# Causal attention: the running maxima of 128 and 256 columns taken for four or two heads in one bank

## Chip, core and metric

One NeuronCore of a Trainium2 chip (trn2) runs the whole program in one launch. The metric is device time in microseconds (us), from the first to the last instruction of the core with what the runtime puts around it. The kernel before took 1778.22 us in the median of 3 runs (1775.87 to 1778.82).

## The reference, cut to what matters

The program is a chain of six layers on x of 4 batches x 1024 tokens x 128 features: a routed feed-forward layer, causal attention, the same feed-forward layer again, a second kind of routed feed-forward layer, a gated attention unit, and that feed-forward layer again. The change is in the causal attention alone:

```
qkv = layernorm(x) @ w_in.T + b_in          # 16 heads of width 8
scores = einsum('bhqd,bhkd->bhqk', q / sqrt(8), k) + causal_bias
attn = softmax(scores, axis=-1)             # exp(score - row maximum) / sum
out = einsum('bhqk,bhkd->bhqd', attn, v) @ w_out.T + b_out
```

The row maximum of each query is needed before the exponentials. The kernel therefore computes the scores twice: once with queries on the partitions, from which VectorE takes the maxima over the keys, and once with keys on the partitions, from which ScalarE takes the exponentials.

## The kernel before, in words

**Sections.** Attention is cut into 16 sections (4 batches x 4 groups of HG = 4 heads). In a section the queries and keys of four heads lie in `q_st` (128 rows of contraction, 1024 queries; the four heads stand in rows of their own) and `k_pad` (one padded copy of the keys for each head j, zero in the other heads' rows). So one stationary tile of 128 queries serves all four heads, and the head is chosen by which `k_pad[:, n % 2, j, ...]` streams past it.

**The maxima (lines 865 to 870, `peak` at 1039 on TensorE and at 1276 on VectorE).** A block (t, c) is the product of query tile t (8 tiles of 128) with key half c (512 keys); only the causal part is computed, `width_of(t, c)` columns: 128, 256, 384 and 512 for t = 0 to 3 and again for t = 4 to 7 in half 1, and 512 for t = 4 to 7 in half 0. That is 12 blocks for each head, 48 in a section. MAXB packs them into 9 PSUM banks for each head, 36 in a section: six blocks stand alone, three banks hold two blocks (128 with 384, twice, and 256 with 256). TensorE issues one weight load and one matmul for each block (line 1049).
**The ring.** These banks, and those of the projections, transposes and the output product, come from a ring of RING = 3 PSUM banks. `fill` (line 978) makes TensorE wait until the bank three entries back has been emptied, `content` (line 985) makes the consumer wait for the fill. Both engines take their instructions strictly in the order of the program.

**The rest of a section.** TensorE also issues the second score products (`score`, line 1068, 12 units of key block and query half for two pairs of heads), the products with v (`pv`, line 1087, two units later), the transposes of the output (`ot`, 1096), and once a batch (four sections) the normalised input's transposes (1013), projections (1019 to 1021), the output transposes (1103) and the output product (`wo`, 1110). ScalarE takes the exponentials (1157), GpSimd zeroes the diagonal (1197). Behind the last maximum of a section VectorE forms the negated maximum in three dependent steps (`neg`, 1294 to 1301), TensorE transposes it (`maxt`, 1058) and a DMA puts it into rows of `q_st`. Once a batch VectorE has the two steps of `wo` (1319 to 1327), each a chain of three operations.

**The order.** `order()` (line 876) gives every step a due time in units of a section and sorts; all engines walk that one list. The maxima of section n run beside the scores of section n - 1 and are spread evenly:

```
put(n - 1.18 + 0.93 * (i * HG + j) / (len(MAXB) * HG), "max", n, j, i)
put(at(g) + pair * weight[u] / sum(weight) / 2, "score", n, u, pair)   # begin[u]: 0, .104, .188, .25, .292, .396, ...
put(at(g + 2) + 0.001, "pv", n, u)
```

The maxima of section 0 have no scores beside them. Those of section 15 are the last; behind them only the scores of section 15 are left.

Of the kernel before, what the change touches and what calls it, by code (L numbers as in the profile page):

```python
# [9 lines left out]
ALU = mybir.AluOpType  # L10
# [838 lines left out]
def phase_attention(nc, k, own, a, begun, lead):  # L849
# [15 lines left out]
    MAXB = (((3, 0),), ((4, 0),), ((5, 0),), ((6, 0),), ((7, 0),), ((0, 0), (2, 0)),  # L865
            ((7, 1),), ((4, 1), (6, 1)), ((1, 0), (5, 1)))
    HALF1 = next(i for i, parts in enumerate(MAXB) if any(c > 0 for _, c in parts))

# [7 lines left out]
    def order():  # L876
# [13 lines left out]
        for n in range(SECTIONS):  # L890
# [14 lines left out]
            for i in range(len(MAXB)):  # L905
                for j in range(HG):
                    put(n - 1.18 + 0.93 * (i * HG + j) / (len(MAXB) * HG), "max", n, j, i)
# [27 lines left out]
    for entry in ORDER:  # L935
        if entry[0] in SMALL:
            if ("max", SECTIONS - 1, HG - 1, len(MAXB) - 1) in SLOT and n % RING == LENT:
                n += 1
            SLOT[entry] = n
            n += 1  # L940
    TAKEN_UP = sum(n % RING == LENT for n in SLOT.values())

    with ExitStack() as ctx:
# [27 lines left out]
        neg_steps, max_in = sem("neg_steps"), sem("max_in")  # L971
# [35 lines left out]
        def _(pe):  # L1007
# [31 lines left out]
            def peak(n, j, i):  # L1039
                bank, full = fill(pe, "max", n, j, i)  # L1040
                at = 0
                if i == 0 and j == 0:
                    pe.wait_ge(q_in[n % 3], 16 * 2 * (n // 3 + 1))
                    pe.wait_ge(k_in[n % 2][0], 16 * HG * (n // 2 + 1))
                if i == HALF1 and j == 0:
                    pe.wait_ge(k_in[n % 2][1], 16 * HG * (n // 2 + 1))
                for t, c in MAXB[i]:
                    width = width_of(t, c)
                    mm = pe.matmul(bank[:, at:at + width], q_st[:, n % 3, t * P:(t + 1) * P],  # L1049
                                   k_pad[:, n % 2, j, c * G:c * G + width], start=True, stop=True,  # L1050
                                   skip_group_check=True)
                    at += width
                mm.then_inc(full, 1)
# [194 lines left out]
        def _(dve):  # L1248
# [27 lines left out]
            def peak(n, j, i):  # L1276
                bank, empty = content(dve, "max", n, j, i)
                if n > 0 and i == 0 and j == 0:
                    dve.wait_ge(neg_steps, 3 * n - 2)
                at = 0  # L1280
                for t, c in MAXB[i]:
                    width = width_of(t, c)
                    now, best = bank[:, at:at + width], mx[:, j, 2 * t + c:2 * t + c + 1]
                    if c == t // TG:
                        ins = dve.tensor_tensor_reduce(now, now, mask[:, G - width:G], 1.0, -3e38, ALU.add, ALU.max, best)  # L1285
                    else:
# [681 lines left out]
```

## Time and profile before

| | before |
|---|---|
| median of 3 runs | 1778.22 us |
| the profiled execution's own time | 1777.67 us |
| its span (first to last instruction) | 1775.7 us |
| attention: first maximum to last exponential product, about | 242 to 830 us |
| TensorE busy | 1644.0 us, 93% of the span |
| VectorE busy | 1289.3 us, 73% |
| ScalarE busy | 1016.6 us, 57% |
| GpSimd busy | 774.5 us, 44% |

A matmul's time in the profile goes from its start to a modelled end and overlaps with the next one's, so a busy TensorE is not one at its peak: the distance from one start to the next (here called the pitch) is what an instruction costs in a row of its kind. The same holds for VectorE, whose instructions overlap a little with the next. The profiled execution lies 0.55 us below the median of the runs.

### The profile page before, as it was taken

To read this page: it belongs to the slowest core of one execution; us is meant where nothing else is said; L and a number is where in the kernel's file an instruction comes from. 1 tells how busy PE (TensorE), PEld (TensorE's weight loads), DVE (VectorE), ACT (ScalarE), POOL (GpSimd) and SP (SyncE) were. 2 spreads that over 40 slices of the span, in tenths; PEclk is the share of its full clock that TensorE was granted. 3 is DMA by queue.
4 is the path that set the end of the run, shared out by engine and by line. 5 is a ranking of instruction groups with operands and counts; after the bars stand their busy time and mean duration, and the time that the engine had idled before them with its cause. 6 is when DMAs were issued, how large, how long until landed. Compare 5 with 4: busy or idle time off the path is not lost. (4 is left out here: it accounts for less than half of the span.)

```text
span 1775.7 us, 25917 instructions
## 1 busy us (share of the span) xinstructions
PE 1644.0 (93%) x8360; PEld 1149.7 (65%) x8360; DVE 1289.3 (73%) x3879; ACT 1016.6 (57%) x1718; POOL 774.5 (44%) x734
## 2 busy tenths in 40 slices
PE   3999879899999999998999999999998988999998
PEld 2777645555555555554777767777777876777776
DVE  4777668788778878883777767777766876767775
ACT  3666415565566566566666645555555645555554
POOL 1566611311311311212566646555574615555555
PEclk9999969999999999999999999999999998999999
DMA  4222211011111111101233332111110002111120
GB/s 149 74 91 84 93 33 35 16 24 25 21 30 24 20 22 28 30 11 38 79 121 120 103 95 88 54 49 48 49 48 1 1 1 90 60 55 60 55 94 19
DMA packets 58246, 95.01 MB, mean 54 GB/s; under 512 B 9312, under 2 KB 17120, under 8 KB 58112
## 3 DMA queue, kind: packets, MB, share of 16 engines
q1 hardware_dynamic: 56000, 91.07, 18.2%
q10 hardware_dynamic: 2112, 2.30, 0.4%
q8 instruction: 66, 1.08, 0.3%
q14 instruction: 68, 0.56, 0.1%
HBM read 76.76 MB, written 2.88 MB: 45 GB/s over the span
## 5 line engine op out<-in xcount | busy, mean ns | idle before, releaser
L695 DVE TENSOR_TENSOR big<-banks,big 128x512 f32<-128x512 f32 x384 | 264.4, 689 | 214.7 <-ACT banks L632 179.8
L1157 ACT ACTIVATE big<-banks 128x1024 f32<-128x1024 f32 (+3 forms) x384 | 304.3, 810 | 187.9 <-PE banks L1068 182.5
L632 ACT ACTIVATE banks<-banks 128x512 f32<-128x512 f32 x384 | 224.0, 583 | 277.3 <-PE banks L575 272.1
L705 DVE TENSOR_TENSOR big<-big,banks 128x512 f32<-128x512 f32 x400 | 274.7, 687 | 29.8 <-PE banks L578 15.9
L1049 PE MATMUL banks<-arena 128*128 128x512 f32 (+3 forms) x768 | 251.9, 407 | 32.2 <-DVE att_mx L1285 15.4
L1285 DVE CUSTOM_DVE_ANT_0 banks<-banks,att_mask 128x128 f32<-128x128 f32 (+3 forms) x512 | 235.6, 521 | 52.2 <-PE banks L1049 51.6
L1197 POOL TENSOR_SCALAR_AFFINE_SELECT big<-big 128x512 f32<-128x512 f32 x128 | 81.2, 635 | 402.5 <-ACT big L1157 402.5
L1049 PEld LDWEIGHTS banks<-arena 128*128 128x128 f32 x768 | 136.6, 199 | 162.3 <-issue 98.2
L665 POOL TENSOR_TENSOR ffn1b_hid_l<-big,ffn1b_hid_h 128x512 fp32r<-128x512 f32 x128 | 165.5, 1293 | 128.3 <-ACT ffn1b_hid_h L637 128.3
L665 POOL TENSOR_TENSOR ffn1a_hid_l<-big,ffn1a_hid_h 128x512 fp32r<-128x512 f32 x128 | 165.2, 1291 | 118.0 <-ACT ffn1a_hid_h L637 118.0
L575 PE MATMUL banks<-xh,arena 128*128 128x512 f32 x512 | 208.7, 408 | 7.9 <-PEq L1451 6.8
L578 PE MATMUL banks<-xh,arena 128*128 128x512 f32 x512 | 203.2, 397 | 0.0
L1068 PE MATMUL banks<-arena 128*128 128x512 f32 (+3 forms) x768 | 200.7, 351 | 2.0 <-ACT big L1157 1.8
L1287 DVE TENSOR_REDUCE att_mx<-banks 128x1 f32<-128x512 f32 x256 | 164.1, 683 | 26.3 <-PE banks L1049 26.2
L1087 PE MATMUL banks<-big,att_v_aug 128*32 128x512 f32 (+3 forms) x1536 | 165.8, 504 | 0.6 <-POOL big L1197 0.5
L1068 PEld LDWEIGHTS banks<-arena 128*128 128x128 f32 x768 | 136.4, 191 | 24.2 <-ACT big L1157 9.2
L665 POOL TENSOR_TENSOR ffn0a_hid_l<-big,ffn0a_hid_h 128x512 fp32r<-128x512 f32 x72 | 92.7, 1289 | 85.6 <-ACT ffn0a_hid_h L637 85.5
L665 POOL TENSOR_TENSOR ffn0b_hid_l<-big,ffn0b_hid_h 128x512 fp32r<-128x512 f32 x72 | 93.0, 1291 | 63.5 <-ACT ffn0b_hid_h L637 62.9
L575 PEld LDWEIGHTS banks<-xh,arena 128*128 128x128 f32 x512 | 97.3, 190 | 29.5 <-issue 8.7
L578 PEld LDWEIGHTS banks<-xh,arena 128*128 128x128 f32 x512 | 97.0, 189 | 22.3
L578 PE MATMUL banks<-xl,arena 128*128 128x512 f32 x256 | 101.7, 397 | 0.0
L575 PE MATMUL banks<-xl,arena 128*128 128x512 f32 x256 | 101.1, 395 | 0.0
(256 smaller groups left out, 3153.7 us busy)
## 6 DMA issues: line engine op xcount, KB each, us to landing
big<-weight_rows SPq DMA_DIRECT2D x256, 128.0 KB, 3.0
big<-weight_rows SPq DMA_DIRECT2D x128, 256.0 KB, 4.3
arena<-att_parts SPq DMA_DIRECT2D x16, 384.0 KB
arena<-att_parts SPq DMA_DIRECT2D x128, 48.0 KB
w_raw<-in_ffn_w_dram SPq DMA_DIRECT2D x12, 256.0 KB, 3.0
out_dram<-x SPq DMA_DIRECT2D x8, 256.0 KB, 2.3
setup_raw<-in_ffn_w_dram SPq DMA_DIRECT2D x3, 576.0 KB, 6.9
gau_angle<-in_consts_dram SPq DMA_DIRECT2D x2, 512.0 KB, 7.3
```

The costliest lines, as they stand in the source:

```text
L575: mm = pe.matmul(gate_ps[:, num % NB, :], w[:, ws], xx[:, g % 2, :], start=m == 0, stop=m == 2)
L578: mm = pe.matmul(up_ps[:, num % NB, :], w[:, ws], xx[:, g % 2, :], start=m == 0, stop=m == 2)
L632: act.activation(gate if c < NSCALED else sil, gate, ACT.Silu).then_inc(silu_done, 1)
L665: pool.tensor_tensor(hid_l[:, num % NH, :], hid[:, num % NH, :], hid_h[:, num % NH, :].bitcast(F32), ALU.subtract).then_inc(low_cut, 1)
L695: dve.tensor_tensor(scl[:, num % 2, :], gate_ps[:, num % NB, :], share[:, c // PER, :], ALU.mult)\
L705: dve.tensor_tensor(hid[:, num % NH, :], scl[:, num % 2, :] if c < NSCALED else sil, up_ps[:, num % NB, :], ALU.mult).then_inc(hidden, 1)
L1049: mm = pe.matmul(bank[:, at:at + width], q_st[:, n % 3, t * P:(t + 1) * P], k_pad[:, n % 2, j, c * G:c * G + width], start=True, stop=True ...
L1068: mm = pe.matmul(score_ps[:, pair, h, 0:c], k_pad[:, n % 2, 2 * pair + h, kb * P:(kb + 1) * P], q_st[:, n % 3, (qg + 1) * G - c:(qg + 1) * ...
L1087: mm = pe.matmul(o_ps[32 * j:32 * j + 32, G - c:G], v_aug[:, b % 2, kb, at:at + 32], probs[:, unit % NPROB, j, 0:c], start=kb == 0, stop=k ...
L1157: act.activation(probs[:, unit % NPROB, 2 * pair:2 * pair + 2, 0:c], score_ps[:, pair, :, 0:c], ACT.Exp, scale=SCALE).then_inc(exped, 1)
L1285: ins = dve.tensor_tensor_reduce(now, now, mask[:, G - width:G], 1.0, -3e38, ALU.add, ALU.max, best)
L1287: ins = dve.tensor_reduce(best, now, AX.X, ALU.max)
```

## The change

Every MAXB entry is now one block for a set of heads: one head (ONE), two (TWO) or all four (ALL). The blocks of 128 columns are taken for all four heads at once (4 x 128 = 512 columns), those of 256 for two heads at once, those of 384 and 512 for each head alone. TensorE issues one matmul for an entry, whose moving operand runs over the heads' copies of the keys. VectorE treats one-head entries as before. A merged entry gets two operations: `tensor_tensor` adds the mask to the last 128 columns of each head in place in the bank, and after a wait on its own semaphore `edged` one `tensor_reduce` over the whole bank gives the maxima of all its heads. A section has 38 entries (32 of one head, 4 of two, 2 of four) in place of 36 banks, in a new order, evenly spread again over 0.93 of a section. `neg` waits for the last three entries.

```diff
--- before.py
+++ after.py
@@ -862,9 +862,12 @@
     LOW, AGAIN = (1, 2), (2, 1)
 
 
-    MAXB = (((3, 0),), ((4, 0),), ((5, 0),), ((6, 0),), ((7, 0),), ((0, 0), (2, 0)),
-            ((7, 1),), ((4, 1), (6, 1)), ((1, 0), (5, 1)))
-    HALF1 = next(i for i, parts in enumerate(MAXB) if any(c > 0 for _, c in parts))
+    ONE, TWO, ALL = [(j, j + 1) for j in range(HG)], [(j, j + 2) for j in range(0, HG, 2)], [(0, HG)]
+    MAXB = [(t, c, heads) for t, c, sets in
+            ((3, 0, ONE), (4, 0, ONE), (5, 0, ONE), (0, 0, ALL), (6, 0, ONE), (1, 0, TWO), (7, 0, ONE), (2, 0, ONE),
+             (7, 1, ONE), (4, 1, ALL), (6, 1, ONE), (5, 1, TWO)) for heads in sets]
+    MERGED = sum(b - a > 1 for _, _, (a, b) in MAXB)
+    HALF1 = next(i for i, (_, c, _) in enumerate(MAXB) if c > 0)
 
     def width_of(t, c):
         return min(G, (t + 1) * P - c * G)
@@ -903,8 +906,7 @@
             for h in range(HALF):
                 put(n - 1.34 + 0.34 * h, "keys", n, h)
             for i in range(len(MAXB)):
-                for j in range(HG):
-                    put(n - 1.18 + 0.93 * (i * HG + j) / (len(MAXB) * HG), "max", n, j, i)
+                put(n - 1.18 + 0.93 * i / len(MAXB), "max", n, i)
             put(n - 0.255, "neg", n)
             put(n - 0.15, "maxt", n)
             for u in range(NU):
@@ -934,7 +936,7 @@
     SLOT, n = {}, 0
     for entry in ORDER:
         if entry[0] in SMALL:
-            if ("max", SECTIONS - 1, HG - 1, len(MAXB) - 1) in SLOT and n % RING == LENT:
+            if ("max", SECTIONS - 1, len(MAXB) - 1) in SLOT and n % RING == LENT:
                 n += 1
             SLOT[entry] = n
             n += 1
@@ -968,7 +970,7 @@
         emptied = [sem(f"emptied{n}") for n in range(RING)]
         moments, eps_done, rstd_done, norm_done = begun.moments, begun.eps_done, begun.rstd_done, begun.norm_done
         xh_done, qk_high, qk_again = sem("xh_done"), sem("qk_high"), sem("qk_again")
-        neg_steps, max_in = sem("neg_steps"), sem("max_in")
+        neg_steps, max_in, edged = sem("neg_steps"), sem("max_in"), sem("edged")
         q_in = [sem(f"q_in{p}") for p in range(3)]
         k_in = [[sem(f"k_in{p}{h}") for h in range(HALF)] for p in range(2)]
         scored, exped, masked = sem("scored"), sem("exped"), sem("masked")
@@ -1036,21 +1038,18 @@
                 bank, full = fill(pe, "proj", b, w, h)
                 three(bank, full, w_h[:, w, :], w_l[:, w, :], h)
 
-            def peak(n, j, i):
-                bank, full = fill(pe, "max", n, j, i)
-                at = 0
-                if i == 0 and j == 0:
+            def peak(n, i):
+                bank, full = fill(pe, "max", n, i)
+                t, c, (j0, j1) = MAXB[i]
+                if i == 0:
                     pe.wait_ge(q_in[n % 3], 16 * 2 * (n // 3 + 1))
                     pe.wait_ge(k_in[n % 2][0], 16 * HG * (n // 2 + 1))
-                if i == HALF1 and j == 0:
+                if i == HALF1:
                     pe.wait_ge(k_in[n % 2][1], 16 * HG * (n // 2 + 1))
-                for t, c in MAXB[i]:
-                    width = width_of(t, c)
-                    mm = pe.matmul(bank[:, at:at + width], q_st[:, n % 3, t * P:(t + 1) * P],
-                                   k_pad[:, n % 2, j, c * G:c * G + width], start=True, stop=True,
-                                   skip_group_check=True)
-                    at += width
-                mm.then_inc(full, 1)
+                width = width_of(t, c)
+                pe.matmul(bank[:, 0:(j1 - j0) * width].rearrange("p (j w) -> p j w", w=width),
+                          q_st[:, n % 3, t * P:(t + 1) * P], k_pad[:, n % 2, j0:j1, c * G:c * G + width],
+                          start=True, stop=True, skip_group_check=True).then_inc(full, 1)
 
             def maxt(n):
                 bank, full = fill(pe, "maxt", n)
@@ -1273,24 +1272,30 @@
                 dve.scalar_tensor_tensor(parts[:, w, LOW[w], cut], bank, b_in[:, w:w + 1], parts[:, w, 0, cut].bitcast(F32),
                                          ALU.add, ALU.subtract).then_inc(empty, 1)
 
-            def peak(n, j, i):
-                bank, empty = content(dve, "max", n, j, i)
-                if n > 0 and i == 0 and j == 0:
+            def peak(n, i):
+                bank, empty = content(dve, "max", n, i)
+                t, c, (j0, j1) = MAXB[i]
+                if n > 0 and i == 0:
                     dve.wait_ge(neg_steps, 3 * n - 2)
-                at = 0
-                for t, c in MAXB[i]:
-                    width = width_of(t, c)
-                    now, best = bank[:, at:at + width], mx[:, j, 2 * t + c:2 * t + c + 1]
-                    if c == t // TG:
-                        ins = dve.tensor_tensor_reduce(now, now, mask[:, G - width:G], 1.0, -3e38, ALU.add, ALU.max, best)
-                    else:
-                        ins = dve.tensor_reduce(best, now, AX.X, ALU.max)
-                    at += width
+                width = width_of(t, c)
+                now = bank[:, 0:(j1 - j0) * width].rearrange("p (j w) -> p j w", w=width)
+                best = mx[:, j0:j1, 2 * t + c]
+                if c == t // TG and j1 - j0 == 1:
+                    ins = dve.tensor_tensor_reduce(bank[:, 0:width], bank[:, 0:width], mask[:, G - width:G], 1.0, -3e38,
+                                                   ALU.add, ALU.max, best)
+                elif c == t // TG:
+                    edge = now[:, :, width - P:width]
+                    dve.tensor_tensor(edge, edge, mask[:, G - P:G].unsqueeze(1).broadcast_to([P, j1 - j0, P]), ALU.add)\
+                       .then_inc(edged, 1)
+                    dve.wait_ge(edged, n * MERGED + 1 + sum(b - a > 1 for _, _, (a, b) in MAXB[:i]))
+                    ins = dve.tensor_reduce(best, now, AX.X, ALU.max)
+                else:
+                    ins = dve.tensor_reduce(best, bank[:, 0:width], AX.X, ALU.max)
                 ins.then_inc(empty, 1)
 
             def neg(n):
-                for j in range(HG):
-                    drained(dve, "max", n, j, len(MAXB) - 1)
+                for i in range(len(MAXB) - RING, len(MAXB)):
+                    drained(dve, "max", n, i)
                 dve.tensor_reduce(nm[:], mx[:].rearrange("p j (t c) -> p (j t) c", c=HALF), AX.X, ALU.max, negate=True)\
                    .then_inc(neg_steps, 1)
                 dve.wait_ge(neg_steps, 3 * n + 1)
```

## Rows read from the trace of the kernel before

**Rows 1.** page of the profile: span, and busy time and instructions of each engine

```profile
span 1775.7 us, 25917 instructions
...
PE 1644.0 (93%) x8360; PEld 1149.7 (65%) x8360; DVE 1289.3 (73%) x3879; ACT 1016.6 (57%) x1718; POOL 774.5 (44%) x734
```

**Rows 2.** by stretch: busy us (x) per engine, clock, DMA share, GB/s

```profile
242.00:267.00 25.00, 24.88 (x50) 13.45 (x50) 23.99 (x80) 0.00 (x0) 0.00 (x0) 0.50 0.18 32
...
736.00:800.00 64.00, 61.51 (x398) 35.50 (x402) 52.65 (x171) 39.46 (x54) 9.87 (x16) 1.00 0.10 18
```

**Rows 3.** waits in 340 to 760: who for whom, us in total, times, longest

```profile
ACT big L1157 <- PE banks L1068: 137.9, 158, 3.6
...
PEld banks L1049 <- DVE att_mx L1285: 22.9, 46, 3.0
...
PE banks L1049 <- DVE att_mx L1285: 10.6, 28, 2.7
```

**Rows 4.** page, costliest groups: lines 1049, 1285 and 1287

```profile
L1049 PE MATMUL banks<-arena 128*128 128x512 f32 (+3 forms) x768 | 251.9, 407 | 32.2 <-DVE att_mx L1285 15.4
L1285 DVE CUSTOM_DVE_ANT_0 banks<-banks,att_mask 128x128 f32<-128x128 f32 (+3 forms) x512 | 235.6, 521 | 52.2 <-PE banks L1049 51.6
...
L1287 DVE TENSOR_REDUCE att_mx<-banks 128x1 f32<-128x512 f32 x256 | 164.1, 683 | 26.3 <-PE banks L1049 26.2
```

**Rows 5.** timeline, VectorE, first section: start us, us, engine line op

```profile
245.44 9.65 DVE L1287 TENSOR_REDUCE att_mx<-banks 128x1 f32<-128x512 f32 x16
...
255.74 0.33 DVE L1285 CUSTOM_DVE_ANT_0 banks<-banks,att_mask 128x128 f32<-128x128 f32 x1
...
255.98 0.59 DVE L1285 CUSTOM_DVE_ANT_0 banks<-banks,att_mask 128x384 f32<-128x384 f32 x1
...
264.06 0.46 DVE L1285 CUSTOM_DVE_ANT_0 banks<-banks,att_mask 128x256 f32<-128x256 f32 x1
...
264.44 0.46 DVE L1285 CUSTOM_DVE_ANT_0 banks<-banks,att_mask 128x256 f32<-128x256 f32 x1
```

**Rows 6.** timeline, VectorE, the negation behind the first section

```profile
267.26 0.18 DVE L1299 CAST att_mst<-att_nm 128x32 fp32r<-128x32 f32 x1
267.48 0.19 DVE L1301 TENSOR_TENSOR att_mst<-att_nm,att_mst 128x32 fp32r<-128x32 f32 x1
267.60 0.70 DVE L1285 CUSTOM_DVE_ANT_0 banks<-banks,att_mask 128x512 f32<-128x512 f32 x1
```

**Rows 7.** groups by shape in 318 to 900: two-operand reads of PSUM

```profile
L1313 DVE TENSOR_TENSOR att_o_tok<-banks,att_rec 128x128 f32<-128x128 f32 x30 | 8.7, 291 | 1.0
...
L1319 DVE TENSOR_TENSOR att_y<-banks,att_bo 128x512 f32<-128x512 f32 x8 | 5.5, 689 | 1.8 <-PE banks L1110 1.8
```

**Rows 8.** timeline, TensorE, two banks of 128 and 384 columns and what follows

```profile
785.62 0.63 PE L1068 MATMUL banks<-arena 128*128 128x512 f32 x2
786.09 0.75 PE L1049 MATMUL banks<-arena 128*128 128x128 f32 x4
786.68 0.63 PE L1068 MATMUL banks<-arena 128*128 128x512 f32 x2
```

**Rows 9.** timeline, last maxima, 776 to 780: VectorE and TensorE

```profile
776.53 4.38 DVE L1287 TENSOR_REDUCE att_mx<-banks 128x1 f32<-128x512 f32 x7 [0.30 <-PE banks L1049]
...
777.93 0.43 PE L1087 MATMUL banks<-big,att_v_aug 128*32 128x128 f32 x8
...
778.28 0.50 PE L1049 MATMUL banks<-arena 128*128 128x512 f32 x1
...
778.62 0.51 PE L1068 MATMUL banks<-arena 128*128 128x384 f32 x2
...
778.97 0.70 PE L1049 MATMUL banks<-arena 128*128 128x512 f32 x2
...
779.51 0.40 PE L1068 MATMUL banks<-arena 128*128 128x256 f32 x2
...
779.84 1.07 PE L1087 MATMUL banks<-big,att_v_aug 128*32 128x512 f32 x8
```

## The prediction

> **What bounds the kernel now.** I read the page first: TensorE 93% busy, VectorE 73% [rows 1]. The change touches attention alone, so I next read stretches of it. In the last full sections TensorE is busy 61.5 of 64 us, VectorE 52.7 [rows 2]. In the first stretch, 242 to 267, VectorE is busy 24.0 of 25 us and the clock granted to TensorE is 0.50, its lower level of 1.2 GHz: these are the maxima of section 0, with nothing else to do, and VectorE sets their pace. Third, the waits [rows 3]: over 12 sections VectorE makes TensorE's weight load at line 1049 wait 22.9 us and its matmul 10.6 (partly the same time), at most 3.0 us at once, and ScalarE waits 137.9 us for score products. So beyond section 0 the end is set by TensorE's ordered list of work; VectorE counts where its backlog reaches TensorE through the ring of three banks. The page gives 768 products, 512 masked and 256 plain maxima [rows 4], which is 48, 32 and 16 for each of 16 sections.
>
> **Removed from and added to VectorE.** The pitches come from section 0, where VectorE never rests [rows 5]: 16 plain maxima of 512 in 9.65 us, 0.60 each; a masked maximum of 128 columns 255.98 - 255.74 = 0.24; one of 256 columns 264.44 - 264.06 = 0.38. The accumulator read lies within these pitches. A merged bank replaces four of 0.24 (0.96) or two of 0.38 (0.76) by an addition, a wait on it, and a maximum of 512. What the wait costs is seen behind section 0 [rows 6]: a cast starts at 267.26 and takes 0.18, and the operation that waits for it starts at 267.48, 0.04 after its end; the next one, which doesn't wait, starts at 267.60, 0.07 before the end of its predecessor (267.48 + 0.19). So a waited operation costs its full duration plus 0.04. The addition reads PSUM and a second operand like the rows of line 1319 (689 ns for 512 elements) and 1313 (291 ns for 128) [rows 7]; 512 elements cost 0.69, 256 by interpolation 0.42. The old kernel has no tensor_tensor that writes back to PSUM; the masked maximum does (0.33 for 128 with a pitch of 0.24), so I bound the new addition by its pitch alone, 0.60, and by 0.80. I take the durations, the nearest rows.
> - Four heads: 0.69 + 0.04 + 0.60 = 1.33 for 0.96: +0.37, twice a section.
> - Two heads: 0.42 + 0.04 + 0.60 = 1.06 for 0.76: +0.30, four times.
> - Together +1.9 us a section, 31 us of VectorE in the kernel, although it issues 44 operations for 48. Every merged bank is read twice; before, one pass did both.
>
> In section 0 this stands on the path: **+1.9 us**.
>
> The Trainium skill (VectorE: DVE Perf Modes, section "The DRAIN you can't avoid") says that a semaphore between chained operations costs nothing, as the pipe is emptied either way. By it the waited addition would cost its pitch, 0.60, and the merged banks 0.13 less each, 12 us of the 31. The rows differ from it here: without a wait the next operation starts before the end, with one after it [rows 6].
>
> **Removed from TensorE.** The columns are the same. Ten weight loads and matmuls a section go. A load is mostly hidden under the matmul before it; it shows where that matmul has 128 columns. Two banks of 128 and 384 take 786.68 - 786.09 = 0.59 [rows 8]; the same 1024 columns in 512s go at 0.23 each (two of them from 785.62 to 786.09), so 0.46. That is 0.065 for each of eight such banks: -0.5 us a section. Where two blocks of 256 are joined the load was hidden; I count nothing, between 0 and 0.1 each. Bounds for the section: -0.3 to -0.9. **Over 15 sections -8 us** (in section 0 VectorE hides it). The two additional banks add no columns; their fill waits are free where the bank is empty. The moving operand with a stride between heads has no row; I take the plain pitch and bound it by nothing and by 0.1 us a merged bank. No DMA, queue or instruction of ScalarE or GpSimd is touched, and the masks added are the same elements.
>
> **The new wait.** A bank of 1.33 us stands in a cadence of 0.93/38 of a section of some 36 us, 0.88 us a bank. Evenly spread, three banks would cover that. The order is not even in TensorE's time, though. By the due times the four-head entry i = 12 falls at n - 0.886, its followers at -0.862, -0.837 and -0.813; pv of unit 11 is due at -0.895, score (1, pair 1) at -0.854 and score (2, pair 0) at -0.8125. So between two products with v stand four entries (12 to 15) and one score pair. Before, three stood there [rows 9]: after pv at 777.93 a bank at 778.28, scores 778.62, two banks at 778.97, scores 779.51, pv 779.84. VectorE at this place is already behind: seven plain maxima without a pause from 776.53, of which the first four are entries 8 to 11, so it is free for entry 12 at 776.53 + 4 x 0.60 = 778.93. With the change: addition from 778.93, maximum from 779.66 to 780.35, bank released about 780.4. TensorE comes to entry 15, which needs that bank, at 778.28 + 0.34 (entry 12) + 0.23 (13) + 0.35 (scores) + 0.23 (14) = 779.43. It waits **1.0 us**, and the scores and pv behind it wait too, then ScalarE for the scores. The bounds are 0 and 1.4 (the whole bank exposed).
>
> At the two-head entries 17 and 18 the products with v and the transposes stand between, and the same bookkeeping gives some 0.3 us at entry 23. The second four-head entry (i = 31) has a pv and an output transpose two entries behind it, a cover of 1.6 us: I cost it at nothing; without that cover it would cost 0.4. Against that, four banks in a row of 0.76 each, which now cost up to 0.3, are thinned out: -0.3. Net **+1.0 us a section, +15 us over 15 sections**, half of it given back by the loads. In three sections the two `wo` chains hold VectorE up (the waits of up to 3.0 us, [rows 3]) and the four-head entry 31 falls right behind: +0.5 each, +1.5. Against this, waiting TensorE lets ScalarE get ahead, so small waits of `pv` for exponentials go: up to -0.3 a section, of which I take 0.2, -3.
>
> **Sum.** +1.9 - 8 + 15 + 1.5 - 3 = +7.4 or so; with the unseen cost of the strided operand and of the write to PSUM (0.1 on each of 96 merged banks at half exposure, +5 at most, +2 taken) **+9.5 us**. The profiled execution of 1777.67 becomes 1787.2; the median is 0.55 higher, so 1787.7.
>
> **Rivals.**
> - *VectorE has room and hides its part.* The ring takes up the long banks because entry 12 isn't late enough; only section 0 pays. For it: VectorE rests 18% of the last sections [rows 2]. Against: seven maxima in a row without rest at just this place [rows 9]. It gives +1.9 - 8 = -6: about 1772. Chance 0.14.
> - *The parts cancel*: the new wait is about 0.5 rather than 1.0, and the total ends within 3.6 us of before. Chance 0.13.
> - *VectorE becomes the bound.* If after each merged bank its lateness is never made up, each section pays the full 1.9, and the saved loads vanish under the wait: 16 x 1.9 = +31, 1809. It decides once TensorE waits at most banks, as it does now in section 0 alone. Against: VectorE's pitches sum to some 27 us of 36. Chance 0.10.
> - *Fewer operations are cheaper by themselves.* From 0.24 at 128 and 0.38 at 256 the fixed part of a masked maximum is 0.10; if the merged forms saved that and had no second pass to pay (an addition and maximum overlapping freely), 4 operations x 0.10 x 16 = -6, with the loads -14: 1764. Chance 0.04. The Trainium skill (VectorE: DVE Perf Modes, section "Rules for kernel authors") speaks for this rival with its advice to minimise the count of operations, not the semaphores.
>
> **How the numbers follow.** The forecast itself (slower by 4 to 25 us) has 0.59. About 0.2%, 3.6 us, is what a measurement of this kernel tells from no change. Faster 0.18 (the first and last rival), same 0.13, slower 0.69 (forecast and VectorE as the bound). The range goes from 1772.5, near the first rival, to 1802, where the upper bounds of wait and addition meet; 0.1 is left out at either side.
>
> **What would show it right or wrong.** In the changed profile: 608 products and 608 loads at the maximum's product line in place of 768; 256 masked maxima left, 96 additions, 352 plain maxima; the additions near 0.69 and 0.42 us, and the maximum behind each starting 0.04 after it; section 0 from 25 to about 27 us; VectorE's busy time up by some 20 us or more; a wait of TensorE near 1 us for the four-head maximum once a section. If those waits are absent and a section is 0.5 us shorter, the first rival holds; if additions overlap the maxima, the last; if TensorE waits at most banks, the third.

## Result: slower by 1.4%, and the profile after

The changed kernel takes **1803.7 us** in the median of 4 runs (1802.26 to 1804.24) against 1778.5, the median of 4 runs of the kernel before on this occasion; the ratio is 1.0136, with an interval of 1.0124 to 1.0149. Its profiled execution took 1803.2 us with a span of 1801.5. I had said 1787.7 with a range up to 1802: right in sign, too small by 16 us, and outside the range.

From the page of the changed kernel, to be read against [rows 1] and [rows 4] (line 1050 is the maxima's product, 1284 the masked maximum of one head, 1293 the plain one):

```profile
span 1801.5 us, 25261 instructions
...
PE 1651.5 (92%) x8200; PEld 1132.6 (63%) x8200; DVE 1321.0 (73%) x3559; ACT 1018.0 (57%) x1718; POOL 776.5 (43%) x734
...
L1050 PE MATMUL banks<-arena 128*128 128x512 f32 (+1 forms) x608 | 257.0, 471 | 48.1 <-DMA arena<-att_parts 14.8
...
L1293 DVE TENSOR_REDUCE att_mx<-banks 128x1 f32<-128x512 f32 x256 | 163.0, 684 | 36.2 <-PE banks L1050 35.9
L1284 DVE CUSTOM_DVE_ANT_0 banks<-banks,att_mask 128x512 f32<-128x512 f32 (+1 forms) x256 | 154.5, 647 | 35.2 <-PE banks L1050 34.6
```

The counts are those expected: 608 products for 768, 256 masked maxima. VectorE is busy 31.7 us longer (1321.0 - 1289.3), although it issues 320 operations less; the forecast was 31. Its share of the span is unchanged, which shows how little such a share says.

Where did the time go? In each trace I took the time from the first product of a maximum to the last score product (start to start), here called **attention**: 590.0 us before, 614.3 after, +24.3. What lies outside is 1185.6 and 1187.2 us, and in the traces of eleven other versions it scatters between 1184.9 and 1191.3 without a pattern. So attention is compared below beside the medians. Inside it, section 0 (up to the first score) grows from 29.5 to 31.6, and a plain section, one without projections or output products beside it, from 32.2 to 33.6.

A section repeats to a few tenths of a us from trace to trace, but only where TensorE's granted clock is the same. In the stretches of the scores of sections 1, 5 and 9 TensorE stands idle once for 2.2 to 2.7 us, waiting for VectorE. Behind that the granted clock falls in some of them to its lower level of 1.2 GHz, for 3.4 or 6.8 us. The changed kernel shows it in section 9 and not in section 5, behind the same wait. (The last two lines give a stretch, its length, busy us and count of TensorE, its loads, VectorE, ScalarE and GpSimd, then the clock, 1.00 and 0.50, the DMA share and GB/s.)

```profile
475.44 0.50 PE L1050 MATMUL banks<-arena 128*128 128x512 f32 x1 [2.18 <-DVE att_mx L1284]
475.77 0.63 PE L1067 MATMUL banks<-arena 128*128 128x512 f32 x2
476.33 1.06 PE L1086 MATMUL banks<-big,att_v_aug 128*32 128x512 f32 x8
...
626.01 0.51 PE L1050 MATMUL banks<-arena 128*128 128x512 f32 x1 [2.18 <-DVE att_mx L1284]
626.35 0.61 PE L1067 MATMUL banks<-arena 128*128 128x512 f32 x2
626.89 1.56 PE L1086 MATMUL banks<-big,att_v_aug 128*32 128x512 f32 x8
...
475.40:478.80 3.40, 3.36 (x17) 1.62 (x17) 2.59 (x9) 1.25 (x2) 3.30 (x4) 1.00 0.02 5
627.34:630.74 3.40, 3.40 (x14) 1.90 (x7) 1.70 (x6) 0.99 (x2) 3.40 (x5) 0.50 0.00 0
```

Section 5 lasts 37.6 us there and section 9 lasts 39.1, so 3.4 us at the lower level cost about 1.5. The traces differ in how much of this they caught, and the differences between them in attention are out by up to 6 us for it. The table below has the time at the lower level from the first score on, and attention less 0.45 us for each us of it, which is an estimate from these two sections, good to 1 or 2 us, and called "at equal clock" from here on.

The waits of the changed kernel in 340 to 760, to be held against [rows 3]:

```profile
PEld banks L1050 <- DVE att_mx L1284: 27.5, 59, 2.6
...
PEld banks L1050 <- DVE att_mx L1291: 13.4, 14, 1.1
PE banks L1050 <- DVE att_mx L1291: 8.3, 14, 0.7
```

Line 1291 is the maximum over a merged bank. It ends 14 waits of up to 1.1 us, a little over one for each section in the stretch. That is the wait that was forecast, and it can be seen in full in the last section with maxima. Timeline of TensorE and VectorE there, start us, us, engine, line, operation (entries 12 and 13, scores (1, 1), entries 14 and 15, scores (2, 0), pv):

```profile
799.57 0.42 PE L1086 MATMUL banks<-big,att_v_aug 128*32 128x128 f32 x8
799.93 0.72 PE L1050 MATMUL banks<-arena 128*128 128x512 f32 x2
800.46 0.70 DVE L1288 TENSOR_TENSOR banks<-banks,att_mask 128x512 f32<-128x512 f32 x1
800.49 0.52 PE L1067 MATMUL banks<-arena 128*128 128x384 f32 x2
800.85 0.40 PE L1050 MATMUL banks<-arena 128*128 128x512 f32 x1
801.19 0.69 DVE L1291 TENSOR_REDUCE att_mx<-banks 128x4 f32<-128x512 f32 x1
801.80 1.28 DVE L1293 TENSOR_REDUCE att_mx<-banks 128x1 f32<-128x512 f32 x2
801.94 0.50 PE L1050 MATMUL banks<-arena 128*128 128x512 f32 x1 [0.69 <-DVE att_mx L1291]
802.27 0.40 PE L1067 MATMUL banks<-arena 128*128 128x256 f32 x2
802.60 0.64 PE L1086 MATMUL banks<-big,att_v_aug 128*32 128x512 f32 x4
```

Entry 14 starts at 800.85. Entry 15 could follow 0.23 later, but its bank is the one that the maximum begun at 801.19 releases at 801.88 (801.19 + 0.69), so it starts at 801.94: 0.86 us of wait, and the scores behind it stand too.

VectorE's prices, from section 0 of the same trace (answers to [rows 5, 6]):

```profile
248.98 0.69 DVE L1288 TENSOR_TENSOR banks<-banks,att_mask 128x512 f32<-128x512 f32 x1
249.71 0.69 DVE L1291 TENSOR_REDUCE att_mx<-banks 128x4 f32<-128x512 f32 x1
250.32 2.47 DVE L1293 TENSOR_REDUCE att_mx<-banks 128x1 f32<-128x512 f32 x4
252.71 0.42 DVE L1288 TENSOR_TENSOR banks<-banks,att_mask 128x256 f32<-128x256 f32 x1
253.16 0.69 DVE L1291 TENSOR_REDUCE att_mx<-banks 128x2 f32<-128x512 f32 x1
```

A four-head bank costs 250.32 - 248.98 = 1.34 us, a two-head bank 1.06 (0.45 to the maximum and 0.61 more); the maximum starts 0.03 to 0.04 after the end of the addition it waits for. Right behind a masked maximum the addition takes 0.73 and 0.47 in place of 0.69 and 0.42.

To see where a section loses time, I compared the start of each score product with its start in the kernel before, both counted from the section's first score. This is a plain section (the maxima of section 14 beside the scores of 13), in us; a score is named (unit, pair of heads). The three columns behind that are attention, the time at the lower clock and the estimate of attention without it. All versions of the experiments below stand in it.

| version | (2,0) | (4,1) | (6,0) | (7,0) | (9,1) | (10,0) | next section | attention | at 1.2 GHz | estimate |
|---|---|---|---|---|---|---|---|---|---|---|
| before | 0 | 0 | 0 | 0 | 0 | 0 | 0 | 590.0 | 15.7 | 583 |
| changed | +1.0 | +0.9 | +0.3 | +0.8 | +0.7 | +1.4 | +1.4 | 614.3 | 13.5 | 608 |
| e1_reads | +0.6 | +0.6 | -0.1 | +0.5 | +0.3 | +1.0 | +1.0 | 603.6 | 11.6 | 598 |
| e2_shift | -0.2 | 0.0 | -0.6 | -0.7 | -0.1 | -0.1 | +0.2 | 594.7 | 7.4 | 591 |
| e3_entry15 | -0.2 | 0.0 | -0.6 | -0.1 | -0.2 | +0.5 | +0.5 | 599.7 | 7.3 | 596 |
| e4_split | +1.1 | +1.1 | +0.4 | +1.0 | +0.9 | +1.5 | +1.6 | 616.2 | 13.5 | 610 |
| e5_entry3 | +1.0 | +0.9 | +0.3 | +0.8 | +0.8 | +0.8 | +1.0 | 605.6 | 7.0 | 602 |
| e6_entry32 | +1.0 | +0.9 | +0.3 | +0.2 | +0.8 | +1.5 | +1.5 | 613.6 | 10.7 | 609 |
| e7_both | -0.2 | -0.1 | -0.7 | -0.8 | -0.2 | -0.2 | +0.1 | 590.9 | 11.4 | 586 |
| e8_old_entry3 | 0.0 | 0.0 | 0.0 | 0.0 | 0.0 | +0.7 | +0.4 | 595.8 | 15.9 | 589 |
| e9_tuned_reads | -0.2 | -0.1 | -0.7 | -0.8 | -0.9 | -1.0 | -0.7 | 578.3 | 5.1 | 576 |
| e10_tuned_passes | -0.2 | 0.0 | -0.6 | -0.7 | -0.5 | -0.7 | -0.4 | 584.7 | 2.6 | 584 |
| e11_tuned_split | 0.0 | +0.1 | -0.5 | -0.4 | -0.5 | -0.5 | -0.2 | 584.3 | 5.3 | 582 |

The changed kernel has three steps: +1.0 before score (2,0), +0.5 before (7,0), +0.7 before (10,0), and one gain of 0.6 between (4,1) and (6,0). The first is entry 15. The others were not in the forecast. At all three places the sorted list shows the same thing. With 38 entries in place of 36, entry 3 is due at -1.1066 of a section and score (10,0) at -1.1042; entry 15 at -0.8129 and score (2,0) at -0.8125; entry 32 at -0.3968 and score (7,0) at -0.3958. In the kernel before, the corresponding bank came just behind. The margins are 0.0004 to 0.0024 of a section, 0.01 to 0.09 us. This gave two theories. **Passes**: VectorE's second reading costs 1.87 us in each section, wherever it stands. **Order**: the loss is at these three places, where one maximum more stands ahead of scores and pv, and the ring of three makes TensorE wait. A third reading, that the change as a whole lowered TensorE's clock, is out: the changed kernel was at the lower level for less time than the kernel before (13.5 and 15.7 us).

### The profile page after: what moved, and what is told of

Its sections match the earlier page's. It is cut to its first block and busy times, and to the rows that moved or that the text cites. A ratio compares the mean times of both kernels' runs of the same rounds, so it can differ in the third digit from the quotient of the medians.

```text
span 1801.5 us, 25261 instructions
## 1 busy us (share of the span) xinstructions
PE 1651.5 (92%) x8200; PEld 1132.6 (63%) x8200; DVE 1321.0 (73%) x3559; ACT 1018.0 (57%) x1718; POOL 776.5 (43%) x734
## 3 DMA queue, kind: packets, MB, share of 16 engines
q8 instruction: 65, 1.06, 0.2%
## 5 line engine op out<-in xcount | busy, mean ns | idle before, releaser
L1050 PE MATMUL banks<-arena 128*128 128x512 f32 (+1 forms) x608 | 257.0, 471 | 48.1 <-DMA arena<-att_parts 14.8
L1050 PEld LDWEIGHTS banks<-arena 128*128 128x128 f32 x608 | 113.1, 198 | 197.8 <-issue 98.5
L665 POOL TENSOR_TENSOR ffn1a_hid_l<-big,ffn1a_hid_h 128x512 fp32r<-128x512 f32 x128 | 165.4, 1293 | 118.6 <-ACT ffn1a_hid_h L637 118.6
L1067 PE MATMUL banks<-arena 128*128 128x512 f32 (+3 forms) x768 | 202.1, 349 | 2.0 <-ACT big L1156 1.8
L1284 DVE CUSTOM_DVE_ANT_0 banks<-banks,att_mask 128x512 f32<-128x512 f32 (+1 forms) x256 | 154.5, 647 | 35.2 <-PE banks L1050 34.6
L1067 PEld LDWEIGHTS banks<-arena 128*128 128x128 f32 x768 | 141.9, 191 | 27.8 <-ACT big L1156 9.2
L665 POOL TENSOR_TENSOR ffn0b_hid_l<-big,ffn0b_hid_h 128x512 fp32r<-128x512 f32 x72 | 93.1, 1293 | 63.3 <-ACT ffn0b_hid_h L637 62.6
```

What stands on the lines that cost most here:

```text
L665: pool.tensor_tensor(hid_l[:, num % NH, :], hid[:, num % NH, :], hid_h[:, num % NH, :].bitcast(F32), ALU.subtract).then_inc(low_cut, 1)
L1050: pe.matmul(bank[:, 0:(j1 - j0) * width].rearrange("p (j w) -> p j w", w=width), q_st[:, n % 3, t * P:(t + 1) * P], k_pad[:, n % 2, j0:j1, ...
L1067: mm = pe.matmul(score_ps[:, pair, h, 0:c], k_pad[:, n % 2, 2 * pair + h, kb * P:(kb + 1) * P], q_st[:, n % 3, (qg + 1) * G - c:(qg + 1) * ...
L1284: ins = dve.tensor_tensor_reduce(bank[:, 0:width], bank[:, 0:width], mask[:, G - width:G], 1.0, -3e38, ALU.add, ALU.max, best)
```

## Experiments

### The second pass taken away, the order kept

```diff
-                    edge = now[:, :, width - P:width]
-                    dve.tensor_tensor(edge, edge, mask[:, G - P:G].unsqueeze(1).broadcast_to([P, j1 - j0, P]), ALU.add)\
-                       .then_inc(edged, 1)
-                    dve.wait_ge(edged, n * MERGED + 1 + sum(b - a > 1 for _, _, (a, b) in MAXB[:i]))
-                    ins = dve.tensor_reduce(best, now, AX.X, ALU.max)
+                    for j in range(j0, j1):
+                        part = bank[:, (j - j0) * width:(j - j0 + 1) * width]
+                        ins = dve.tensor_tensor_reduce(part, part, mask[:, G - width:G], 1.0, -3e38, ALU.add, ALU.max,
+                                                       mx[:, j, 2 * t + c:2 * t + c + 1])
```

> The changed kernel, but VectorE takes a merged bank apart again: one masked maximum for each head, as before; TensorE's merged products and the new order stay. Theory 'passes' (the second pass over each merged bank, +1.87 us a section as section 0 shows, comes through in full): about 1803.7 - 30 = 1774. Theory 'order' (the loss is at three places where the new list puts one bank more ahead of scores or pv, entries 3, 15 and 32): section 0 gives 1.9 back, the wait at entry 15 falls from 1.0 to about 0.6, those at 3 and 32 stay: 1803.7 - 1.9 - 15 x 0.5 = 1794.

1792.4 us, ratio 1.0076 (1.0059 to 1.0093); attention 603.6, 10.7 less than the changed kernel. Section 0 gives 1.9 of it back; the four 128-column maxima take 0.96 there:

```profile
252.69 0.29 DVE L1289 CUSTOM_DVE_ANT_0 banks<-banks,att_mask 128x128 f32<-128x128 f32 x1
...
253.65 2.48 DVE L1292 TENSOR_REDUCE att_mx<-banks 128x1 f32<-128x512 f32 x4
```

The wait at entry 15 falls from 1.0 to 0.6, and the other two steps stay. With VectorE's operations exactly as they were before the change, the kernel is still 14 us slower. "Passes" alone is out; "order" named 1794.

### The order mended, the second pass kept

```diff
-                put(n - 1.18 + 0.93 * i / len(MAXB), "max", n, i)
+                put(n - 1.18 + 0.93 * i / len(MAXB) + 0.004, "max", n, i)
```

> The changed kernel with every maximum due 0.004 of a section later, which in a plain section moves three entries and nothing else: entry 3 behind score (10, 0) and pv 8, entry 15 behind score (2, 0) and pv 0, entry 32 behind score (7, 0), pv 5 and an output transpose. Theory 'order': the steps of about 0.7, 1.0 and 0.6 us at these places go, up to 2.3 us a section; with some given back elsewhere 1.3 to 1.6: 1780 to 1784. Theory 'passes': VectorE has as much to do as before, so the time stays within 4 us of 1803.7.

1784.95 us, ratio 1.0034 (1.0019 to 1.0048); attention 594.7. A constant of 0.004 sections, some 0.15 us, takes 19.6 of the 24.3 us away, without one instruction more or less (18.7 in the median, 17 by the estimate at equal clock). The value lies 1 us above the range that "order" gave and 15 below that of "passes". The same place as above, in this version:

```profile
783.01 0.43 PE L1086 MATMUL banks<-big,att_v_aug 128*32 128x128 f32 x8
783.36 0.73 PE L1050 MATMUL banks<-arena 128*128 128x512 f32 x2
783.90 0.70 DVE L1288 TENSOR_TENSOR banks<-banks,att_mask 128x512 f32<-128x512 f32 x1
783.93 0.51 PE L1067 MATMUL banks<-arena 128*128 128x384 f32 x2
784.28 0.39 PE L1050 MATMUL banks<-arena 128*128 128x512 f32 x1
784.51 0.39 PE L1067 MATMUL banks<-arena 128*128 128x256 f32 x2
784.63 0.69 DVE L1291 TENSOR_REDUCE att_mx<-banks 128x4 f32<-128x512 f32 x1
784.84 1.06 PE L1086 MATMUL banks<-big,att_v_aug 128*32 128x512 f32 x8
```

VectorE's 1.34 us are there unchanged (783.90 to 785.24, where the next one starts). Scores (2,0) and pv now stand ahead of entry 15 and cover them: from one pv to the next 1.83 us pass (783.01 to 784.84), with the wait 3.03 (799.57 to 802.60), of which 0.23 are the entry itself.

### The three places one by one

```diff
-                put(n - 1.18 + 0.93 * i / len(MAXB), "max", n, i)
+                put(n - 1.18 + 0.93 * i / len(MAXB) + 0.004 * (i == 15), "max", n, i)
```

The two other runs have 3 or 32 in place of 15.

> The changed kernel with entry 15 alone 0.004 of a section later, behind score (2, 0) and pv 0. The wait of about 1.0 us that the prediction worked out for this entry then has 1.2 us of TensorE's work in front of it. Theory 'order': -1.0 x 15 = -15 at most, and -5 at least, since 0.7 us of this step is given back by the middle of the section as it is. Theory 'passes': the lateness turns up at the next places, change under 4 us.

1789.4 us, ratio 1.0062 (1.0044 to 1.0080); attention 599.7, 14.6 less. The median falls by 14.3, and the estimate at equal clock says 12. The first step is gone and doesn't come back later: what was lost there was lost for the section.

> The changed kernel with entry 3 alone 0.004 of a section later, behind score (10, 0) and pv 8. Entries 0 to 3 are masked maxima of 512 for one head, which the change leaves as they were. Theory 'order': the step of 0.6 to 0.8 us at the end of a section goes, in the 13 sections that have one, 0.3 of it is given back elsewhere already: attention 4 to 8 us shorter than in the changed kernel, 1796 to 1799. Rival: the step comes from a backlog of the longer merged banks before it (entries 36 and 37) and stays: within 3 us of 1803.7.

1797.8 us, ratio 1.0107 (1.0083 to 1.0131); attention 605.6, 8.7 less, a little more than expected; the median falls by 5.9, and the estimate at equal clock by 6. The step before (10,0) is gone, and 0.4 of it is still gone where the next section starts. This one has nothing to do with a merged bank: entries 0 to 3 are masked maxima of one head.

> The changed kernel with entry 32 alone 0.004 of a section later, behind score (7, 0), pv 5 and an output transpose. Theory 'order': the step of 0.6 us in the middle of a section goes; with what the entry shift together gave (19 us for three, 14 of them from entry 15) 1 to 4 us less than the changed kernel. Rival: the wait turns up at entry 34, which needs the four-head bank 31: no change.

1801.1 us, ratio 1.013 (1.0112 to 1.0149); attention 613.6, 0.7 less. The median falls by 2.6, which is in the range of "order", but the runs scatter by 5 and the estimate at equal clock shows no gain. The trace decides: as the rival said, the wait turns up at entry 34. The step moves from (7,0) to (7,1), where entries 32, 33 and 34 now stand three in a row. The bank that entry 34 needs is not the four-head bank 31, though, but that of the output transpose that stands behind entry 31, and VectorE empties it after bank 31. The original place shows what three in a row cost; the row of three lasts until the scores at 781.95, 1.24 us for 0.23 + 0.23 + 0.18:

```profile
780.71 1.41 PE L1050 MATMUL banks<-arena 128*128 128x512 f32 x3
781.95 0.63 PE L1067 MATMUL banks<-arena 128*128 128x512 f32 x2
```

In attention the three single shifts sum to 24.0 us, and made together they give 19.6. The changed kernel's own trace enters all three and has a stretch at the lower clock in section 12 that the others lack; by the estimates at equal clock the shifts sum to 17 (12, 6 and -1) and give 17 together, so they are independent as far as this resolves.

### The same fault put into the kernel before

```diff
-put(n - 1.18 + 0.93 * (i * HG + j) / (len(MAXB) * HG), "max", n, j, i)
+put(n - 1.18 + 0.93 * (i * HG + j) / (len(MAXB) * HG) - 0.003 * (i == 0 and j == 3), "max", n, j, i)
```

> The kernel before, with nothing merged, but bank 3 of a section (the fourth masked maximum of 512) due 0.003 of a section earlier, so that it goes ahead of score (10, 0) and pv 8 as in the changed kernel. Theory 'order': the step at the end of a section, 0.6 us, appears here too: attention 4 to 9 us longer than before, 1783 to 1787. Rival: the step belongs to the merged banks, no change: 1776 to 1781.

1783.6 us, ratio 1.0025 (1.0013 to 1.0038); attention 595.8, +5.8 us, with the same time at the lower clock. The step of 0.7 before (10,0) appears in a kernel with nothing merged, and the next section gives 0.3 of it back. Its timeline, TensorE (two banks ahead of scores (10,0)):

```profile
774.32 0.59 PE L1068 MATMUL banks<-arena 128*128 128x384 f32 x2
775.07 1.15 PE L1049 MATMUL banks<-arena 128*128 128x512 f32 x2 [0.17 <-DVE att_mx L1285]
776.05 0.40 PE L1068 MATMUL banks<-arena 128*128 128x256 f32 x2
```

Two products of 512, entries 2 and 3, take 0.98 us here (775.07 to 776.05) for 0.46. The third place of the ring holds the transposed maxima (`maxt`, 1058), so entry 3 waits for the bank of entry 1, the second of two masked maxima of 0.62 to 0.65 us that VectorE had only just been given. The changed kernel has the same rows:

```profile
790.66 0.59 PE L1067 MATMUL banks<-arena 128*128 128x384 f32 x2
791.42 1.15 PE L1050 MATMUL banks<-arena 128*128 128x512 f32 x2 [0.16 <-DVE att_mx L1284]
792.41 0.39 PE L1067 MATMUL banks<-arena 128*128 128x256 f32 x2
```

### Both mended

The edits of e1_reads and e2_shift together.

> The changed kernel with the merged banks read head by head by VectorE (as in the first run) and all maxima due 0.004 later (as in the second). TensorE's merged products stay. Theory 'order and passes' (the two explain the loss between them): attention lasts 590 us as before the change or 2 us less, 1774 to 1779. Rival: something else of the change costs time, the moving operand with a stride or the two additional banks: 1781 or more.

1780.35 us, ratio 1.0002 (0.9988 to 1.0017); attention 590.9, against 590.0 before the change. Median and attention are about a us over what I expected and below what the rival asked for (at equal clock attention is 3 us over the kernel before, 1 to 2 by the medians). So beyond the order and the second pass the rest of the change comes out near nothing in sum. This doesn't take the sum apart: a cost of the strided moving operand or of the two additional banks could be hidden by the loads saved. With the mended list the second pass is worth 594.7 - 590.9 = 3.8 us (5 at equal clock), 1.9 of them in section 0; with the change's own list it was 10.7 (10). The table shows one step left, 0.6 between (7,0) and (9,1): the three in a row.

### No three in a row, with and without the second pass

```diff
-                put(n - 1.18 + 0.93 * i / len(MAXB) + 0.004, "max", n, i)
+                put(n - 1.18 + 0.93 * i / len(MAXB) + 0.004 + 0.006 * (i == 34) + 0.012 * (i == 36), "max", n, i)
```

> The run with both edits (merged products, VectorE head by head, all maxima due 0.004 later), and in addition entries 34 and 36 later by 0.006 and 0.012, behind score (7, 1) and behind score (8, 0) with pv 6, so that nowhere three maxima stand in a row. The trace of that run has a step of 0.6 us a section left between scores (7, 0) and (7, 1). Theory 'order': it goes, 0.3 to 0.6 us in 15 sections, attention 582 to 587 us, the whole 5 to 9 us below the run with both edits: 1771 to 1776, under both kernels. Rival: VectorE is merely later for the next entries, nothing gained: 1778 to 1782.

**1770.5 us**, ratio 0.9954 (0.9941 to 0.9967): faster than both kernels, and just under what was expected. Attention lasts 578.3 us, 4 below the range given for it, because this trace was at the lower clock for 5.1 us only. Of the 11.7 us that it is shorter than before the change, 7 are left at equal clock; the medians differ by 8. Against e7_both it is 10 us at equal clock and in the medians, so clearing the rows of three is worth more than any single shift but that of entry 15.

> The same list, but VectorE reads the merged banks twice as the change has it. In the two pairs so far this cost attention 10.7 us with the change's own list and 3.8 with the shifted one, of which 1.9 in section 0 each time. Theory 'order and passes': 2 to 6 us more than its twin without the second pass. Theory 'passes alone': 28 us more, 16 x 1.87 less nothing.

1776.2 us, ratio 0.9995 (0.9983 to 1.0007); attention 584.7, 6.4 over its twin (5.7 in the median, 8 at equal clock), just above the range of "order and passes" and far below the 28 of "passes alone". The change as written, with its list mended, is level with the kernel before; VectorE's 31 us of additional work show as 6 to 8.

### What the merged products are worth

```diff
-                pe.matmul(bank[:, 0:(j1 - j0) * width].rearrange("p (j w) -> p j w", w=width),
-                          q_st[:, n % 3, t * P:(t + 1) * P], k_pad[:, n % 2, j0:j1, c * G:c * G + width],
-                          start=True, stop=True, skip_group_check=True).then_inc(full, 1)
+                for j in range(j0, j1):
+                    mm = pe.matmul(bank[:, (j - j0) * width:(j - j0 + 1) * width], q_st[:, n % 3, t * P:(t + 1) * P],
+                                   k_pad[:, n % 2, j, c * G:c * G + width], start=True, stop=True,
+                                   skip_group_check=True)
+                mm.then_inc(full, 1)
```

In the changed kernel:

> The changed kernel, but TensorE fills the merged banks with one load and one product for each head, as before; VectorE and the order are unchanged. It prices the saved loads alone. The prediction's step: +0.5 us in each of 15 sections, +8 us, 1811. Rival: loads lie under TensorE's waits for VectorE, no change within 3 us.

1804.2 us, ratio 1.0143 (1.0127 to 1.0159): no difference in the median, attention 616.2, +1.9 with the same time at the lower clock. In the fastest version:

> The fastest version so far (merged products, VectorE head by head, the list without three maxima in a row) with one load and one product for each head again: 48 in place of 38 a section, order and VectorE unchanged. It prices the merged products where TensorE waits least for VectorE. The prediction's price: 8 banks x 0.065 us x 15 sections = 8 us more, 1778. Rival, from the same edit in the changed kernel, which made attention 1.9 us longer: the loads lie under waits, 0 to 3 us more, 1770 to 1774.

1775.8 us, ratio 0.999 (0.9977 to 1.0003), so 5 us over its twin; attention 584.3, +6.0, or 0.4 a section, 0.05 for each of its eight blocks of 128 columns. The median lies between the two that were expected, the forecast price's 1778 and the rival's 1770 to 1774. The load that shows behind a short product is real, nearly at the forecast price of 0.065, and what the strided operand costs is already taken off. In the changed kernel only a third of it shows: splitting the products there shortens the wait before entry 15 from 1.08 to 1.03 us and moves score (2,0) by 0.1, where in the fastest version, which has no wait there, it moves by 0.2.

## Why the prediction was wrong, step by step

**VectorE's prices: right.** 1.33 and 1.06 were forecast for the merged banks, 1.34 and 1.06 measured; +1.9 us in section 0, measured +1.86 (from the start of the first maximum to the end of the last, 23.99 us become 25.85) and +2.1 up to the first score; +31 us of VectorE in all, measured 31.7. The Trainium skill (VectorE: DVE Perf Modes, section "The DRAIN you can't avoid") would have had the waited maximum start at the pitch of 0.60 that the prediction took for the addition; it starts after 0.73, so here the measurement goes against the rule.

**The new wait at entry 15: right**, in place, cause and size (1.0 forecast, 0.9 to 1.0 in the sections looked at), and worth 12 to 15 us as e3_entry15 shows, for the 15 in the sum. Of the step of 1.0, e1_reads leaves 0.6 with each bank read in one pass: most of it is the fourth entry in the row, the rest the second pass.

**"The second four-head entry ... I cost it at nothing": wrong.** There is a step of 0.5 to 0.6 here. I looked for a wait on the long bank 31, found it covered, and passed over entry 32, which needs bank 29 and stands third in a row. The long bank isn't needed for it: e1_reads has the same step. Clearing the rows of three later gave 10 us (e9_tuned_reads against e7_both, both with the three places mended).

**Entry 3: a step that the prediction doesn't have.** I had worked through the due times only around merged banks. Going from 36 to 38 entries moves every due time, and the fourth one-head masked bank slipped ahead of scores (10,0): +0.7 at that place, 0.4 left of it in the next section, 6 us in all (8.7 in the trace of e5_entry3, 5.9 in its median), and 5.8 in the old kernel when only this is done to it. The sentence "Evenly spread, three banks would cover that. The order is not even in TensorE's time, though" was the right warning, used at one place out of three.

**The `wo` sections, +1.5: right in size, wrong in what [rows 3] shows.** Sections 4 and 8, which have the `wo` steps, grow by 1.9 us where plain ones grow by 1.4 to 1.5, and entry 33, which needs the four-head bank 31, waits 0.90 us in sections 4, 8 and 12. But the waits of up to 3.0 us in the kernel before, which the prediction gave to the `wo` chains, stand in sections 1, 5 and 9. There VectorE has the statistics for the next batch's normalisation between two maxima, for 2.4 us:

```profile
463.40 1.64 DVE L1253 BATCH_NORM_STATS2 att_st<-x 128x6 f32<-128x128 f32 x8
...
465.83 0.29 DVE L1285 CUSTOM_DVE_ANT_0 banks<-banks,att_mask 128x128 f32<-128x128 f32 x1
```

These waits don't grow with the change: TensorE's idle time there goes from 2.66 to 2.18 us.

**"Over 15 sections -8 us": mis-sized.** The unit price holds (6.0 us in e11_tuned_split), but a saved load ahead of a wait mostly makes the wait longer: 1.9 us in the changed kernel. So 6 of the 16 us by which the forecast fell short are here, as much as at entry 3. In the same sum I took -3 for ScalarE getting ahead; no such return shows, the changed kernel's row keeps +0.9 to +1.0 up to score (4,1). The +0.3 at entry 23 doesn't show either. The list did gain 0.6 to 0.7 between (4,1) and (6,0), where the kernel before has three banks of 128 and 384 columns and a load that waits 0.58 us for VectorE (0.27 in the changed kernel); all versions with the new packing have that gain. I had put it at 0.3, in the right direction, and no run takes it apart further. The 2 us for the strided operand and the writes to PSUM were never seen by themselves.

**The rivals.** "VectorE becomes the bound" gave 1809 and lies nearest to 1803.7, for the wrong reason: e2_shift and e10_tuned_passes have the same work on VectorE and take 1785 and 1776. The range was too narrow because it put bounds on the price of every operation, and none on places that the list creates. Single sections stray by more than the table's first columns show. Section 12 lasts 36.4 us before, 39.9 in the changed kernel and 35.8 to 38.2 in the other versions; the granted clock was 0.50 for 3.4 us of it in the changed kernel's trace (757.04 to 760.44) and 1.00 throughout in the others. What decides whether the clock falls there was not looked into.

## What to carry to other kernels

Where an in-order engine is fed by a list sorted by due times and hands work to another through a short ring, price the list as well as the work: write out the sequence before and after, and look for every place where more entries than before stand between two pieces of cover, the unchanged ones too. A shift of 0.15 us in the due times was worth 17 to 20 us here, about three times the whole merging of products. Before a difference between two traces is put down to the list, compare the granted clock of the same sections in both. And merging operations pays on the engine where it saves a fixed cost (a weight load behind a short product); on the one where a fused pass becomes two passes over wider data it doesn't, though the count of operations falls.

## What the runs showed of the hardware

- The saved weight loads: a product of 128 columns is too short to cover the load behind it. Joining four of them saves 0.2 us (the table's (2,0) column, e11_tuned_split against e9_tuned_reads), twice a section; the joined products of 256 columns, two between (2,0) and (6,0) and two before (9,1), add nothing to it (0.23 us at both (4,1) and (6,0), 0.45 to 0.47 from (7,1) on).
- `tensor_tensor` that reads and writes PSUM in place with a broadcast second operand takes 0.69 us for 512 elements, the same as from PSUM into SBUF [rows 7], and 0.42 for 256; the maximum over four heads' rows at once, 0.69, costs as much as over one row of 512.
- In the maxima of section 0 TensorE's granted clock stayed at 0.50, its 1.2 GHz level, in both kernels ([rows 2], and 240.8 to 268.0 after the change). The time there is VectorE's, which is busy 25.99 of 27.20 us, so the lower level cost little if anything:

```profile
240.80:268.00 27.20, 24.47 (x40) 11.46 (x40) 25.99 (x62) 0.00 (x0) 0.00 (x0) 0.50 0.17 29
```
- Behind waits of 2.2 to 2.7 us of TensorE the granted clock fell to 0.50 for 3.4 or 6.8 us in some traces and stayed at 1.00 in others: sections 1, 5 and 9 all show it before the change, none of them in e10_tuned_passes, where they have waits of 2.2 us as well. Eight products with v took 1.56 us from 626.89 on and 1.06 at the full clock.
